# Second layer of six experts: the high activations times high and low weights in one product of 512 columns, with the two halves added on VectorE

## The reference, cut to what matters

```python
router_probs = jax.nn.softmax(tokens @ gate_w, axis=-1)       # 1024 tokens, 8 experts
top_w, top_idx = jax.lax.top_k(router_probs, 2)
for e in range(8):
    hmid  = gelu(tokens @ w1[e] + b1[e])                      # 256 -> 1024
    out_e = hmid @ w2[e] + b2[e]                              # 1024 -> 256
    combined = combined + cw[:, e:e + 1] * out_e              # cw is 0 where e was not chosen
x = x + gb * (combined + hidden_states)
```

## Time and profile before

| What | Value |
|---|---|
| Time, median of 3 runs | 290.25 us (289.51, 290.25, 292.1) |
| Span of the profiled execution | 290.3 us, 4525 instructions |
| TensorE (PE) busy | 274.4 us, 95% |
| VectorE (DVE) busy | 198.6 us, 68% |
| ScalarE (ACT) busy | 179.7 us, 62% |
| GpSimd (POOL) busy | 121.5 us, 42% |
| Granted TensorE clock, mean | 0.970 of full speed |

### The profile page before, as it was taken

The page is one execution under the profiler, slowest core; times in us unless marked ns, Lnnn a source line. Parts: engine busy times, 40 slices in busy tenths (PEclk is TensorE's granted clock), DMA queues, the critical chain, the costliest instruction groups (busy, mean ns, idle before and its releaser), DMA issues.

```text
span 290.3 us, 4525 instructions
## 1 busy us (share of the span) xinstructions
PE 274.4 (95%) x1594; PEld 224.0 (77%) x1594; DVE 198.6 (68%) x465; ACT 179.7 (62%) x297; POOL 121.5 (42%) x99
## 2 busy tenths in 40 slices
PE   7989999999999999999999999999999999999980
PEld 2655555468697888776697888999999999999970
DVE  4489599749739759668777386876776768686520
ACT  4238787774495349926885238958769594949100
POOL 8032300000415014484683406548383838566661
PEclk9979999999999999999997599999999999999997
DMA  6990000000008563244179239639295775717133
GB/s 193 382 302 1 2 1 0 0 2 0 0 2 304 167 186 56 72 128 169 46 235 285 64 121 253 175 85 340 77 291 136 224 207 172 210 21 216 20 42 37
DMA packets 32374, 37.94 MB, mean 131 GB/s; under 512 B 7956, under 2 KB 27980, under 8 KB 32332
## 3 DMA queue, kind: packets, MB, share of 16 engines
q1 hardware_dynamic: 26736, 30.10, 32.7%
q0 software_dynamic: 4928, 7.44, 11.4%
q10 hardware_dynamic: 684, 0.06, 0.2%
HBM read 31.63 MB, written 8.90 MB: 140 GB/s over the span
## 4 chain that ended last, share of the span: by engine, by line
PE 70%; DVE 14%; ACT 5%; issue 4%; DMA 2%; POOL 2%; POOLq 1%; DVEq 0%; ACTq 0%
PE bank L1014 19%; PE bank L1043 15%; PE bank L686 8%; PE bank L611 6%; PE bank L783 5%; PE bank L876 2%; PE bank L995 2%; PE bank L1038 2%; PE bank L1037 2%; DVE u L1554 2%; PE bank L622 2%; PE bank L630 1%; DVE xhat L1457 1%; PE bank L640 1%; DMA x_tok<-in_L_attn_x 1%
## 5 line engine op out<-in xcount | busy, mean ns | idle before, releaser
L2065 POOL DMA_INDIRECT out_x<-y_tok,meta x24 | 49.1, 2047 | 46.7 <-DVE y_tok L1907 28.9
L1043 PE MATMUL bank<-w_hi,own 128*128 128x256 f32 x256 | 51.4, 296 | 0.0
L1043 PEld LDWEIGHTS bank<-w_hi,own 128*128 128x128 f32 x256 | 42.7, 200 | 2.3 <-issue 1.6
L1889 DVE TENSOR_TENSOR own<-own_raw,own 128x256 fp32r<-128x256 f32 x64 | 27.1, 424 | 21.0 <-ACT own L1370 16.5
L1014 PE MATMUL bank<-xe_hi,w_hi 128*128 128x320 f32 x128 | 40.1, 313 | 1.5 <-DVE xe_lo L1860 0.8
L1014 PE MATMUL bank<-xe_lo,w_hi 128*128 128x320 f32 x128 | 39.6, 309 | 0.0
L1014 PE MATMUL bank<-xe_hi,w_lo 128*128 128x320 f32 x128 | 39.5, 309 | 0.0
L1364 ACT ACTIVATE own_raw<-bank,b1c 128x320 f32<-128x320 f32 x64 | 33.9, 530 | 8.1 <-PE bank L1014 7.7
L1043 PE MATMUL bank<-w_lo,own 128*128 128x256 f32 x128 | 37.3, 291 | 0.0
L2055 POOL DMA_INDIRECT gb_rows<-gb_table,meta x24 | 24.4, 1015 | 11.7 <-issue 6.7
L1370 ACT ACTIVATE own<-own_raw 128x320 fp32r<-128x320 f32 x64 | 28.8, 462 | 0.0
(11 more groups left out here) (249 smaller groups left out, 626.0 us busy)
## 6 DMA issues: line engine op xcount, KB each, us to landing
e_raw<-in_L_ffn_w SPq DMA_DIRECT2D x16, 1024.0 KB
x_rows<-in_L_attn_x SPq DMA_DIRECT2D x1, 2560.0 KB
xe_tok<-x_rows SPq DMA_DIRECT2D x7, 256.0 KB
raw_m<-in_L_attn_up_W SPq DMA_DIRECT2D x2, 768.0 KB, 9.9
x_tok<-in_L_attn_x SPq DMA_DIRECT2D x2, 512.0 KB, 5.2
out_x<-x_tok SPq DMA_DIRECT2D x1, 1024.0 KB, 5.2
wmod<-in_L_wmod SPq DMA_DIRECT2D x1, 768.0 KB, 11.9
raw_m<-in_L_attn_down_W SPq DMA_DIRECT2D x1, 768.0 KB, 12.6
```

Of the source, the lines that this page charges most:

```text
L1043: ins = nc.tensor.matmul(bank[b][0:n, 0:D], l, r, start=(c == 0 and t == 0), stop=(c == KE - 1 and t == 2))
L1889: nc.vector.tensor_tensor(own_lo[e % 2][:, f, :], own_raw[:, f % 4, 0:whole], own_hi[e % 2][:, f, 0:whole].bitcast(F32), ALU.subtract)
L2065: nc.gpsimd.indirect_dma_start(out_rows, bass.IndirectOffsetOnAxis(ap=ids[0:n, e, k, E:E + 1], axis=0), y_tok[e % 2][0:n, k, :], None, com ...
```

## The change

For experts 1 to 6 and the two tiles of 128 rows, the high and low second-layer weights become one tile of 512 columns for each block c. One product of 512 columns takes the high activations through both; a second one of 256 columns adds the low activations times the high weights to the left half. The right half of the bank (columns 256 to 511) then holds high x low. ScalarE copies it to a new tile `wide_rows`, VectorE adds it to the left half, and the scaling step reads the sum. Both steps are added to the engines' written orders. Experts 0 and 7 and the tile of 64 rows stay as they are.

```diff
-            w2_hi.append(at(f"w2_hi{s}", o, [KE, D], F32R))
-            w2_lo.append(at(f"w2_lo{s}", o + EB, [KE, D], F32R))
+            w2_both.append(at(f"w2_both{s}", o, [KE, 2 * D], F32R))
+            w2_hi.append(w2_both[s][:, :, 0:D])
+            w2_lo.append(w2_both[s][:, :, D:2 * D])
...
+        wide_rows = at("wide_rows", o_rbuf + (2 * ST + 1) * D * 4, [D])
+        def wide(e):
+            return 1 <= e < E - 1
...
-                        for t, (l, r) in enumerate(three([g[s][:, c, k * P:k * P + n] for g in (own_hi, own_lo)], (w2_hi[s][:, c, :], w2_lo[s][:, c, :]))):
-                            ins = nc.tensor.matmul(bank[b][0:n, 0:D], l, r, start=(c == 0 and t == 0), stop=(c == KE - 1 and t == 2))
+                        if wide(e):
+                            if c:
+                                nc.tensor.matmul(bank[b][:, 0:D], own_lo[s][:, c, k * P:(k + 1) * P], w2_hi[s][:, c, :], start=False, stop=False)
+                            ins = nc.tensor.matmul(bank[b][:, 0:2 * D], own_hi[s][:, c, k * P:(k + 1) * P], w2_both[s][:, c, :], start=(c == 0), stop=(c == KE - 1))
+                            if c == 0:
+                                nc.tensor.matmul(bank[b][:, 0:D], own_lo[s][:, c, k * P:(k + 1) * P], w2_hi[s][:, c, :], start=False, stop=False)
+                        else:
+                            for t, (l, r) in enumerate(three([g[s][:, c, k * P:k * P + n] for g in (own_hi, own_lo)], (w2_hi[s][:, c, :], w2_lo[s][:, c, :]))):
+                                ins = nc.tensor.matmul(bank[b][0:n, 0:D], l, r, start=(c == 0 and t == 0), stop=(c == KE - 1 and t == 2))
...
+            def keep_wide(e, k):
+                b, base, _ = y_bank(e, k)
+                n = (e - 1) * (ST - 1) + k
+                if n:
+                    act.wait_ge(y_joined, n)
+                act.wait_ge(filled[b], base + 1)
+                nc.scalar.activation(wide_rows[:], bank[b][:, D:2 * D], ACT.Copy).then_inc(wide_kept, 1)
...
                     if e + 2 < E:
                         x_hi(e + 2)
                         w1_hi_of(e + 2)
+                    keep_wide(e, 0)
                     w2_hi_of(e + 1)
+                    keep_wide(e, 1)
...
+                    elif wide(e):
+                        n_wide = (e - 1) * (ST - 1) + k + 1
+                        dve.wait_ge(wide_kept, n_wide)
+                        nc.vector.tensor_tensor(y_tok[e % 2][:, k, :], rows_of_y, wide_rows[:], ALU.add).then_inc(y_joined, 1)
+                        dve.wait_ge(y_joined, n_wide)
+                        rows_of_y = y_tok[e % 2][:, k, :]
```

More of the change, by code:

```diff
@@ L325, in adaln_block @@
         assert 2 * KE * T * 4 + 4 * HB <= 2 * KF * T * 4 + 12 * HB
-        w1_hi, w1_lo, w2_hi, w2_lo = [], [], [], []
+        w1_hi, w1_lo, w2_both, w2_hi, w2_lo = [], [], [], [], []
         for s, o in enumerate((o_wa, o_wm)):
@@ L354, in adaln_block @@
         low_rows = at("low_rows", o_rbuf + 2 * ST * D * 4, [D])
+        wide_rows = at("wide_rows", o_rbuf + (2 * ST + 1) * D * 4, [D])
+        assert (2 * ST + 2) * D * 4 <= 4 * BH * (S + PAD) * 4
+        def wide(e):
+            return 1 <= e < E - 1
         y_tok = [at(f"y_tok{s}", o_rbuf + s * ST * D * 4, [ST, D]) for s in range(2)]
@@ L426, in adaln_block @@
         low_kept, low_joined = sem("low_kept"), sem("low_joined")
+        wide_kept, y_joined = sem("wide_kept"), sem("y_joined")
         eg_hi_done, eg_lo_done = sem("eg_hi_done"), sem("eg_lo_done")
```

## The result

| | Before | After |
|---|---|---|
| Median of 22 runs each, us | 289.67 (286.81 to 293.16) | 290.73 (288.95 to 293.53) |
| Ratio after / before, 95% interval | | 1.0065 [1.0038, 1.0093] |
| Profiled execution: span, us | 290.3 | 290.7 (its run took 292.47) |
| TensorE, VectorE, ScalarE busy, us | 274.4, 198.6, 179.7 | 273.7, 202.7, 184.3 |

The changed kernel is a little slower: 1.06 us by the medians, 0.65% by the ratio, with an interval that leaves out 1. The forecast was 290.2 against 290.25, so no change; the time lies in its range (288.5 to 291.9), but the small loss is real and was not forecast. The ratio leaves out runs that lie over 1.5% above the fastest run of their kernel, seven of before and one of after, and so comes out larger than the difference of the plain means of all 22 runs, which is 1.04 us [0.14, 1.96] or 0.36%.

What follows compares the result with a forecast made beforehand. TensorE was taken to bound the kernel until after expert 6, then VectorE's last tile and GpSimd's scatters. Gain 1.04 in experts 1 to 5 less 0.97 at the end, net -0.07: 290.2 us, range 288.5 to 291.9.

Steps and rivals of the forecast that it cites:

- pairs of 0.347: TensorE, second layers of experts 1 to 6: 512- plus 256-column product replaces three taking 0.360 us, saving 1.25 us in all.
- A: Rival: the whole TensorE gain of 1.25 us arrives, 289.0 us; chance 0.10.
- D: Rival: the mixed pair on TensorE has no fixed part, gaining 3.2 less 0.97, 288.0 us; chance 0.06.
- B: Rival: the wide product saves nothing on TensorE and the end costs 1.1 to 1.8, 291.4 to 292.0 us; chance 0.14.
- E: Rival: operand changes make most of TensorE's fixed 13 ns, so a fifth of the gain arrives, 291.1 us; chance 0.07.
- Costed at nothing: Experts 1 to 5: the added copies and adds fit into idle time of ScalarE, VectorE and bank 6, cost 0.
- Rival C: Middle experts: tile 0's copy starts over 1.2 us late, bank 6 stalls TensorE before tile 2, 294.4 us; chance 0.08.
- +0.97: End, expert 6: ScalarE's copy delays the last weight conversion, subtraction and scatters, so the end comes 0.97 us later.
- follow its tile by 0.27: GpSimd, expert 6: tile 0's scatter starts 0.27 us after its tile is scaled at 270.65, before the subtraction at 271.48.
- "free" form: End: tile 0's scatter of expert 6 starts before VectorE's last big subtraction, end 0.97 later, net -0.07, 290.2 us.
- held form: End: tile 0's scatter starts too late, waits out VectorE's subtraction, end 1.66 us later, net +0.62, 290.9 us.
- the first term of the sum: TensorE gain of experts 1 to 5 from fewer products, 5 x 0.21 = 1.04 us saved.

Runs made afterwards that it cites:

- b3_side: Kernel before's products plus all copies and adds of the changed kernel, the copy taking the left half; 292.02 us, ratio to before 1.0145 (4 runs).
- a4_swap6: Changed kernel, but in expert 6 ScalarE converts expert 7's second-layer weights before it copies tile 0's half; 289.76 us, ratio to before 0.9964.
- a3_only6: Changed kernel with the wide form in expert 6 only, experts 1 to 5 as before; 292.16 us, ratio to before 1.0043.
- a2_first5: Changed kernel with the wide form in experts 1 to 5 only, expert 6 as before; 289.05 us, ratio to before 1.0000.
- c1_held: Changed kernel with two small VectorE fills ahead of the scaling of expert 6's tile 0; 290.99 us, ratio to before 0.9978.
- c2_free: Changed kernel with two small VectorE fills behind the scaling of expert 6's tile 0, ahead of the last big subtraction; 291.61 us, ratio to before 1.0056.
- d1: Kernel before with expert 0's 16 bias products given all 128 rows instead of 8, the added ones zero; 286.13 us, ratio to before 0.9894.
- d3_first5_full: Wide form in experts 1 to 5 only, with the bias products given all 128 rows; 286.00 us, ratio to before 0.9870 (8 runs).
- b1_after: The changed kernel run again without edits; 291.87 us against 289.76 for before, ratio 1.0110 (6 runs).
- d2_after_full: Changed kernel with the bias products given all 128 rows; 287.38 us, ratio to before 0.9929.
- b2_layout: Changed kernel with the 512-column weight tiles only, its products, copies and adds those of the kernel before; 290.6 us, ratio to before 1.0040.
- a0_before: The kernel before, unchanged, run against itself as a yardstick; 290.2 us against 289.78, ratio 1.0018.

## Why the prediction was right and wrong

**TensorE.** Forecast: pairs of 0.347, 0.21 us an expert, periods of 15.64. Shown: 14 blocks, from the product at 265.90 to the one at 270.80, take 4.90 us, so 0.350 each, and the period is 15.71. TensorE in order of time, after:

```profile
265.90 0.40 PE L1052 MATMUL bank<-w_both,own 128*128 128x512 f32 x1
...
270.80 0.40 PE L1052 MATMUL bank<-w_both,own 128*128 128x512 f32 x1
...
272.79 0.78 PE L1045 MATMUL bank<-w_both,own 128*128 128x256 f32 x2
273.40 0.28 PE L1047 MATMUL bank<-w_both,own 128*64 128x256 f32 x1
```

An expert gives 0.14, and five give 0.71 instead of 1.04. The pair takes a little more than the sum of its parts; the direction was right and the term was almost half too large (1.04 against 0.71). For one product fewer, 0.14 / 16 is some 9 ns. The Trainium skill, "TensorE: Matmul & The Clock Gate", section "Wait — 56ns, not 53.3ns?", would have 2.5; the trace lies between that and the 13 of the earlier trace rows, nearer to the 13. A and D (more gain) are out, B (none) and E (a fifth) too.

**The middle.** Costed at nothing, shown by b3_side: periods of 15.85 with all side work and none of the saving. Rival C (bank 6) didn't come. In the period shown of after, ScalarE's copies stand where they were put:

```profile
222.55 0.39 ACT L1400 ACTIVATE wide_rows<-bank 128x256 f32<-128x256 f32 x1 [0.34 <-PE bank L1052]
222.83 1.91 ACT L1296 ACTIVATE w_both<-e_raw 128x2048 fp32r<-128x2048 f32 x1
225.37 0.38 ACT L1400 ACTIVATE wide_rows<-bank 128x256 f32<-128x256 f32 x1 [0.63 <-PE bank L1052]
227.24 0.38 ACT L1392 ACTIVATE low_rows<-bank 64x256 f32<-64x256 f32 x1 [1.49 <-PE bank L1045]
```

3.37 us of idle time ahead of `keep_low` have become 1.49, and TensorE noticed nothing.

**The end.** The mechanism was the one foreseen: copy, `w2_hi_of(7)`, `w2_lo_of(7)`, tile 1, scatters; a4_swap6 confirms that the order in ScalarE's queue delays the subtraction, and the idle stretch of 0.76 ahead of the subtraction was called. Forecast +0.97, shown +1.04 in a3_only6, and TensorE waited for it at no cost: of the two products shown as one at 272.79 the second, expert 7's first, was due at 272.91 and by the next row (273.40 - 0.12) began at 273.28, so 0.37 us, where some 0.3 was forecast. (The prediction's "some 0.2 more" that TensorE loses is 0.1 by its own times, 273.95 against 273.84; nothing hangs on it.) Two steps were wrong. The scatter was to follow its tile by 0.27 and so to start 0.56 us ahead of the subtraction (270.92 against 271.48). It followed by 0.81 here (269.97 to 270.78), as it had in the earlier trace rows, where I had put that down to the running subtraction. Here no subtraction ran in those 0.81 us. In all profiles each expert's first scatter behind a gather starts 0.80 us after its tile is scaled, whether GpSimd had idled 2.2 us (a2_first5) or 7; a scatter that follows another scatter starts 0.27 after what it waited for, even after 2.85 us of idle time (a3_only6, 279.80 to 280.06). So the subtraction is not what makes the 0.8. The rows speak for the gather ahead of it and against the length of the wait, though the one long wait behind a scatter was for a DMA and not for VectorE; the reason is not shown. So the scatter and the subtraction start within 0.04 us of each other, and the "free" form, on which the sum rested, is a race. And the held form costs 0.60 on top (c1_held against c2_free), not 0.69.

**The sum.** -1.04 + 0.97 = -0.07 was forecast; -0.71 + 1.04 = +0.33 by the parts, +0.41 by the whole, and 1.00 when the scatter is held. The step that failed is the first term of the sum, the price of a product: the pair takes 0.350 us and not 0.347, so five experts give 0.71 and not 1.04, and the two terms no longer cancel. Of the 0.48 us between -0.07 and +0.41 this is 0.33. The held form, which I had at +0.62, stands at +1.00.

**What stays open.** The runs show more than the traces. Leaving out the launch with d1 to d3, 28 runs of after stand +1.00 us [0.46, 1.55] above 121 of before; the trace gives 0.41 free and 1.00 held, and all three profiles of this code (after, b1_after, d2_after_full) are free ones. The mean granted clock of a run says where part of it lies. For 99 of these runs of before it is on record too, and a straight line through the times against that clock, with one constant for the changed kernel, puts after +0.43 us [0.04, 0.81] above before at equal clock, an estimate that agrees with the 0.41. The rest goes with the clock: 4 of 28 runs of after have a mean clock of 0.978 or more, against 28 of 99 of before, and none of the 28 lies below 288.5 us, against 28 of 121. The changed products, the copies and the adds come after S, behind the part where the clock differs; the weights' new layout comes before it, but b2_layout, which has it alone, has 3 of 12 runs below 288.5. And c1_held, which differs from after by two small fills, has 4 of 12 runs below 288.5; c2_free has none. So 0.4 us is shown as the cost in the changed code, up to 1.0 where the scatter is held. Whether the changed kernel also gets the full clock less often, or these launches had it less often by chance, is not shown, nor how often an unprofiled execution holds the scatter.

## What to carry to other kernels

Where a change saves a little on the bounding engine in each round and puts a step into another engine's queue, go to the last round: there the queue's next step has no round to hide in, and one delay of 1 us ate five savings of 0.14. The cheapest way to keep such a gain is to leave the last round as it was (a2_first5, d3_first5_full). And before a change of a few tenths of a us, look at the granted clock by stretches: here one edit of the bias products moved the mean by 3.7 us, nine times the 0.41 of this change.

## What the runs showed of the hardware

- A scatter of GpSimd (1.43 to 1.62 us when alone) that starts while VectorE subtracts two SBUF tiles of 2048 columns ends some 1.5 us after the subtraction: it takes 2.9 us when it starts 0.9 into it, 3.71 at 0.08 (c1_held). Shown 0.02 us ahead of the subtraction it took 1.62 (c2_free). Shown 0.04 us behind the subtraction's start it took 1.62 in four profiles and 3.75 in one; where it took 1.62, the subtraction was a little longer (2.36 instead of 2.28, by the rows of after). The Trainium skill, "SBUF — State Buffer", section "Who interferes with whom", infers that making descriptors isn't blocked by such an instruction. The runs show that the scatter as a whole is, 3.71 in c1_held against 1.62 in c2_free. It also reads its row numbers from SBUF (`meta`), and no run here tells which of the two is held.
- An expert's first scatter, which follows a gather, starts 0.8 us after its tile is scaled, with 2.2 to 7 us of idle time before it; a scatter that follows another scatter starts 0.27 to 0.3 us after what it waited for, with up to 2.85 us of idle time.
- Four products with 8 rows in the stationary and the streamed operand take 1.06 us from the first's start to the next product's at full clock, four with 128 rows 0.68, for the same columns.
- TensorE's clock stood at its 1.2 GHz level for 0 to some 10 us between 155 and 167, in different executions of the same instructions. It fell behind the small bias products (12 of 13 profiles; in none of three with 128 rows), and also in or right behind a wait of TensorE of 2.35 us (a0_before) and 3.26 us (d3_first5_full).
